# Second attention: exponentials as f16 halves, turned by transposing DMAs, with scores in three pairs of banks

## The reference, cut to what matters

```
x = x + tanh(g_xattn[1]) * L1(layernorm(x), ctx, ctx, wq, wk, wv)
L1: Q, K, V = split(q @ wq.T), split(k @ wk.T), split(v @ wv.T)     # 16 heads of 32
    scores = einsum('bhqd,bhkd->bhqk', Q, K) / sqrt(32)             # 154 keys, no mask
    out    = einsum('bhqk,bhkd->bhqd', softmax(scores), V)          # no output matrix
```

## Time and profile before

| | us |
|---|---|
| median of 3 runs | 2781.3 |
| the profiled execution | 2809.87 |
| its span, first to last instruction | 2808.1 |
| first maximum of the second attention (line 842) | starts 1651.68 |
| last maximum | starts 1965.54 |
| first matmul of the stage behind | starts 1982.32 |

### The profile page before, as it was taken

How to read it: one execution, slowest core, us unless ns; L and a number is a source line. 1 busy time by engine, 2 the same in 40 slices (tenths; PEclk the granted TensorE clock), 3 DMA queues, 4 the chain that set the end, 5 groups by cost and what they waited for, 6 DMA issues and landing times. The chain is left out here.

```text
span 2808.1 us, 44981 instructions
## 1 busy us (share of the span) xinstructions
PE 2644.7 (94%) x16990; PEld 1473.8 (52%) x16990; DVE 1594.4 (57%) x2629; ACT 1425.9 (51%) x3586; POOL 1042.0 (37%) x823
## 2 busy tenths in 40 slices
PE   5999988999999989999999979999999999999999
PEld 3554544444444457777777645565444444444444
DVE  6888885655555346655656568988543422333222
ACT  3888885323222146666666548999443222322221
POOL 1455451465555636666766500111102201221111
PEclk8999999999999999999999989999999999999999
DMA  6221214222222269999999842321420110011000
GB/s 186 52 85 57 74 31 169 61 61 61 75 70 54 76 215 289 285 296 282 288 288 289 207 101 76 91 44 42 157 64 16 46 42 34 16 46 46 19 12 30
DMA packets 287479, 311.17 MB, mean 111 GB/s; under 512 B 155169, under 2 KB 164129, under 8 KB 287265
## 3 DMA queue, kind: packets, MB, share of 16 engines
q1 hardware_dynamic: 250400, 240.96, 27.0%
q0 software_dynamic: 36864, 67.34, 11.7%
HBM read 198.86 MB, written 75.89 MB: 98 GB/s over the span
## 5 line engine op out<-in xcount | busy, mean ns | idle before, releaser
L1376 POOL DMA_INDIRECT ids<-sh_tk,sh_su x256 | 269.8, 1054 | 243.9 <-PE sh_gu L55 70.5
L55 PE MATMUL ex_gu<-ex_xT,ex_h 128*128 128x256 f16 x3072 | 347.5, 273 | 4.6 <-issue 3.8
L55 PEld LDWEIGHTS ex_gu<-ex_xT,ex_h 128*128 128x128 f16 x3072 | 301.2, 98 | 53.9 <-issue 4.4
L1775 POOL DMA_INDIRECT xp<-ex_oo,ex_to x128 | 242.3, 1893 | 178.6 <-ACT ex_oo L1683 123.2
L2323 POOL TENSOR_TENSOR fe_prodT<-fe_pp,fe_prodT 128x512 f16<-128x512 f32 x64 | 77.5, 1210 | 591.2 <-ACT fe_prodT L2108 591.2
L521 PE MATMUL at_g<-id,at_p 128*128 128x128 f32 x1280 | 205.1, 288 | 38.7 <-POOL at_p L901 30.7
L1510 DVE SCALAR_TENSOR_TENSOR ex_h<-ring,ex_h 128x1024 f16<-128x1024 f32 x128 | 151.1, 1222 | 153.0 <-ACT ex_h L1500 153.0
L521 PEld LDWEIGHTS at_g<-id,at_p 128*128 128x128 f32 x1280 | 164.9, 169 | 106.9 <-issue 41.7
L680 ACT ACTIVATE at_s<-at_s,at_mx 128x154 f32<-128x154 f32 x512 | 210.4, 417 | 0.0
L900 POOL TENSOR_TENSOR at_p<-at_s,at_rs 128x1024 f32<-128x1024 f32 x64 | 121.5, 1898 | 223.3 <-DVE at_rs L800 223.3
L55 PE MATMUL at_g<-hm_zT,hm_w 128*128 128x512 f16 x768 | 182.1, 389 | 19.8 <-issue 12.5
(11 more groups left out here) (331 smaller groups left out, 5407.8 us busy)
## 6 DMA issues: line engine op xcount, KB each, us to landing
ring<-L_ffn_expert_gate_up_w SPq DMA_DIRECT2D x64, 1024.0 KB
ring<-L_ffn_expert_down_w SPq DMA_DIRECT2D x64, 512.0 KB
ring<-x SPq DMA_DIRECT2D x24, 1024.0 KB, 5.8
x<-ring SPq DMA_DIRECT2D x16, 1024.0 KB, 4.7
zrows<-hm_zs SPq DMA_DIRECT2D x32, 256.0 KB
xp<-ring SPq DMA_DIRECT2D x8, 1024.0 KB
out<-ring SPq DMA_DIRECT2D x8, 1024.0 KB, 4.3
ring<-xp SPq DMA_DIRECT2D x7, 1024.0 KB, 5.7
```

Of the source, the lines that this page charges most:

```text
L55: mm = nc.tensor.matmul(out, lhs(a, k), rhs(b, k), start=start and i == 0 and j == 0, stop=stop and i == n - 1 and j == 2)
L1376: e.indirect_dma_start(ids, bass.IndirectOffsetOnAxis(slotu[b % 2][:, t, j:j + 1], 0), pair[b % 2][:, t, j, :], None, bounds_check=SLOTS - ...
L1775: e.indirect_dma_start(dst, bass.IndirectOffsetOnAxis(to[:, n:n + 1], 0), o32[y % 2][:, t, :], None, bounds_check=T + SLOTS - 1, oob_is_er ...
```

## The change

Only the second attention is changed (and the semaphores of the two attentions are two sets now).

- The exponentials go to `sc`, f32, all eight heads straight from PSUM. The copy (844) is gone; both maxima are read from PSUM. Scores go round three pairs of banks; `gen` shrinks from four banks to two.
- VectorE makes the high half, `high(i)`: two copies to f16, 128 x 1024 and 128 x 208. It stands after the maxima of unit i+1 and before that step's pieces.
- GpSimd makes the low half: two subtractions, of 128 x 1024 and 128 x 208, with two SBUF inputs.
- SyncE issues two transposing DMAs for each unit, 128 x 1280 f16 each, straight into `pT`. The ten TensorE transposes of a unit and the three copies from PSUM (690, 860) are gone.
- The values are three f16 terms (high by high, high by low, low by high) instead of one f32 product; V and VR are kept in f16 halves, and all four groups of a block stand in phases 7 and 3, two each.

```diff
-        gen = [ps(f"g{i}", [P, 512]) for i in range(4)]
+        gen = [ps(f"g{i}", [P, 512]) for i in range(4 if L0 else 2)]
+        S = ps("S", [P, HH, 256])
+        pairs = [S[:, HG * i:HG * i + HG, :] for i in range(2)]
+        if not L0:
+            pairs.insert(0, maps_ahead.gen[:, :, :].rearrange("p b (k n) -> p (b k) n", n=256))
+        def scores(i, part):
+            return pairs[(2 * i + part) % len(pairs)]
...
-        VALS, FIN = ((7, 8, 11, 12), (13, 13, 14, 14)) if L0 else ((6, 7, 10, 11), (12, 12, 13, 13))
+        VALS, FIN = ((7, 8, 11, 12), (13, 13, 14, 14)) if L0 else ((7, 7, 11, 11), (12, 12, 13, 13))
...
+                        for i in range(unit - NP, unit):
+                            e.wait_ge(*keys_landed(i))
+                    if not L0:
+                        for hv, hp in TERMS:
+                            for j in range(HG):
+                                o = grp * P + j * HD
+                                e.matmul(out[j * HD:(j + 1) * HD, :], V[g][:, hv, o:o + HD],
+                                         ptb[:, hp, place(gi * HG + j), :], start=(hv, hp) == TERMS[0], stop=False)
+                        for hv, hp in TERMS:
+                            mm = e.matmul(out[:, :], VR[g][:, hv, grp, :], ptb[:, hp, HH + gi, :], start=False,
+                                          stop=(hv, hp) == TERMS[-1])
...
-                        e.wait_ge(s["clip"], i)
-                        if not L0:
-                            e.wait_ge(s["expd"], 2 * i - 1)
+                        e.wait_ge(*((s["clip"], i) if L0 else (s["expd"], 2 * i - 1)))
...
-                e.wait_ge(s["expd"], 2 * UNITS - 1)
+                e.wait_ge(s["expd"], 2 * UNITS)
...
+            def high(i):
+                e.wait_ge(s["expd"], 2 * i + 2)
+                if i >= NP:
+                    e.wait_ge(*keys_landed(i - NP))
+                e.tensor_copy(first_keys(prob[i % NP][:, 0, :]), sc[i % NS][:, :, 0:P])
+                e.tensor_copy(last_keys(prob[i % NP][:, 0, :]), rest_of(i)).then_inc(s["p_hi"], 1)
...
+                if not L0 and 0 <= n - behind < UNITS:
+                    e.wait_ge(s["p_hi"], i + 1)
+                    e.tensor_tensor(first_keys(rows[:, 1, :]), sc[i % NS][:, :, 0:P], first_keys(rows[:, 0, :]), ALU.subtract)
+                    e.tensor_tensor(last_keys(rows[:, 1, :]), rest_of(i), last_keys(rows[:, 0, :]), ALU.subtract
+                                    ).then_inc(s["p_lo"], 1)
...
+            def turn_keys(i):
+                if i % TPB == 0 and i // TPB >= 2:
+                    e.wait_ge(s["o_mm"], 2 * (i // TPB) - 2)
+                t = i % TPB
+                for h, made in enumerate(("p_hi", "p_lo")):
+                    e.wait_ge(s[made], i + 1)
+                    e.dma_start_transpose(pT[i // TPB % 2][:, h, :, t * P:(t + 1) * P], prob[i % NP][:, h, :]
+                                          ).then_inc(s[f"keys{i % NP}"], 16)
```

More of the change, by code:

```diff
@@ L262, in __init__ @@
             self.KTn = [sb(f"KT{g}", [P, KT, CTX]) for g in range(BATCH)]
-            self.V, self.VR = [sb(f"V{g}", [P, D]) for g in range(BATCH)], [sb(f"VR{g}", [P, KT, P]) for g in range(BATCH)]
+            half = lambda n, s_: ctx.enter_context(nc.sbuf_tensor(f"at{layer}_{n}", s_, F16))
+            self.V = [half(f"V{g}", [P, 2, D]) for g in range(BATCH)]
+            self.VR = [half(f"VR{g}", [P, 2, KT, P]) for g in range(BATCH)]
     def tensor_keys(self, g, m, out):
@@ L298, in vector_values @@
             heads = lambda rows: rows.rearrange("p g (h n) -> p g h n", h=HG)
-            out = v.tensor_tensor(heads(self.VR[g][:, :, :]), heads(bank.rearrange("p (g m) -> p g m", g=KT)),
-                                  self.mine[:, None, :, None].broadcast_to([P, KT, HG, HD]), ALU.mult)
-        else:
-            out = v.tensor_copy(self.V[g][:, :], bank)
-        out.then_inc(s["v_out"], 1)
+            rows, mine = (heads(bank.rearrange("p (g m) -> p g m", g=KT)),
+                          self.mine[:, None, :, None].broadcast_to([P, KT, HG, HD]))
+            high, low = (heads(self.VR[g][:, h, :, :]) for h in range(2))
+            v.tensor_tensor(high, rows, mine, ALU.mult).then_inc(s["v_hi"], 1)
+            v.wait_ge(s["v_hi"], 3 * g + 2)
+            v.tensor_tensor(low, rows, high, ALU.subtract).then_inc(s["v_hi"], 1)
+            v.wait_ge(s["v_hi"], 3 * g + 3)
+            v.tensor_tensor(low, low, mine, ALU.mult).then_inc(s["v_out"], 1)
+        else:
+            v.tensor_copy(self.V[g][:, 0, :], bank).then_inc(s["v_hi"], 1)
+            v.wait_ge(s["v_hi"], 3 * g + 1)
+            v.tensor_tensor(self.V[g][:, 1, :], bank, self.V[g][:, 0, :], ALU.subtract).then_inc(s["v_out"], 1)
     def scalar_query(self):
@@ L374, in attention @@
     NX = 5
-    NS = 3 if L0 else 2
+    NS = 3
     NP = 2 if L0 else 3
@@ L490, in keys_of, with first_keys, last_keys, rest_of @@
         def keys_of(pb, j):
-            if L0:
-                return pb[:, j * P:(j + 1) * P]
-            if j < HH:
-                return pb[:, :].rearrange("p (n k) -> p k n", k=HH)[:, j, 0:P]
-            return pb[:, :].rearrange("p (n j) -> p j n", j=HH // HG)[:, j - HH, HG * P:]
+            return pb[:, j * P:(j + 1) * P]
+        def first_keys(rows):
+            return rows[:, 0:HH * P].rearrange("p (h n) -> p h n", h=HH)
+        def last_keys(rows):
+            return rows[:, HH * P:].rearrange("p (j r n) -> p r j n", r=HG, n=HD)[:, :, :, 0:REM]
+        def rest_of(i):
+            return sc[i % NS][:, :, P:CTX].rearrange("p (r j) n -> p r j n", r=HG)
+        def keys_landed(i):
+            return s[f"keys{i % NP}"], 32 * (i // NP + 1)
         def part_out(i, part):
@@ L610, in tensor @@
                     piece(*what)
-                if 0 <= i < UNITS:
-                    if not L0:
-                        e.wait_ge(s["expd"], 2 * i + 2)
+                if L0 and 0 <= i < UNITS:
                     keys_turned(i, 4, 1)
@@ L697, in scalar @@
                         exps(n - lag, part)
-                    if part < by_scalar:
+                    if L0 and part < by_scalar:
                         part_copy(n - behind, part)
@@ L840, in vector @@
                         e.wait_ge(s["clip"], i + 1)
-                    else:
-                        e.tensor_reduce(mx[i % 3][:, halves[0]], Sh[0][:, :, 0:CTX], AX.X, ALU.max,
-                                        negate=True).then_inc(s["neg"], 1)
-                        e.tensor_copy(sc[i % NS][:, :, :], Sh[1][:, :, 0:CTX]).then_inc(s["clip"], 1)
+                    for part, half in enumerate(halves):
+                        e.tensor_reduce(mx[i % 3][:, half], sc[i % NS][:, half, :] if L0 else scores(i, part)[:, :, 0:CTX],
+                                        AX.X, ALU.max, negate=True).then_inc(s["neg"], 1)
+                    if not L0:
                         summed(n - lag - 1)
-                        e.wait_ge(s["clip"], i + 1)
-                    for half in halves if L0 else halves[1:]:
-                        e.tensor_reduce(mx[i % 3][:, half], sc[i % NS][:, half if L0 else slice(0, HG), :], AX.X, ALU.max,
-                                        negate=True).then_inc(s["neg"], 1)
                 else:
@@ L852, in vector @@
                 i = n - behind
+                if not L0:
+                    high(i)
+                    for what in plan[n]:
+                        piece(*what)
+                    continue
                 for part in range(by_scalar, 3):
@@ L963, in sync @@
             for n in range(STEPS):
+                if not L0 and 0 <= n - behind < UNITS:
+                    turn_keys(n - behind)
                 for what in sorted(plan[n], key=lambda what: what[0] != "turn"):
@@ L2392, in program @@
         with ExitStack() as own:
-            A = Attention(nc, own, K, I, 0, ring, at_s, I["x"], homes)
+            A = Attention(nc, own, K, I, 0, ring, at0_s, I["x"], homes)
             def sync_first():
```

76 lines of the change are left out of this document (42 added, 34 removed).

## The result

| | before | after |
|---|---|---|
| median of the runs of one comparison | 2785.6 (4 runs) | 2883.6 (2881.3 to 2886.1, 4 runs) |
| ratio of the medians, 95% interval | | 1.035 [1.032, 1.038] |
| in the profiled execution: first maximum of the second attention | 1651.68 | 1634.65 |
| last maximum | 1965.54 | 2025.08 |
| first matmul of the stage behind | 1982.32 | 2058.30 |

The stage is 93.0 us longer, nearly all of the 98 between the medians. (The spans differ less, 2884.1 against 2808.1: in the profiled execution of before everything ahead of this stage took 17.0 us longer; behind it both take 825.8.) The forecast was +46. Of all executions behind this text one slow one, of e9, is left out: 3406 us at a granted clock of 0.742, where the others of e9 had 0.97.

A forecast was written before the change was run, and what follows sets the result against it. No one engine bounds the kernel; TensorE, ScalarE and VectorE are within 10% of the block. Terms 26 - 2 - 4 + 2 + 1 + 12 + 11 = +46 us on 2781.3 gave 2827; range 2764 to 2872.

The forecast's parts named there:

- VectorE's balance and the short phases: VectorE gains 0.75 us a unit without waits; phases 0 and 1 take 3.6 each, 2 5.45, 6 3.7, 7 4.2.
- The port: Phases 2 to 4: VectorE's pieces take turns with GpSimd's subtraction at a shared port, 7.1 us a block.
- the lock doesn't bite: Rival: GpSimd's start slips behind VectorE's pieces or yields; blocks of 37.65, -11 us in all, 2770; 18%.
- half: Rival: the port lock bites half, no clock loss; about +10 us with the end, 2792; 17%.
- Two banks: Phases 4 and 5: the projection waits for the bank of `finish` 0; they become 10.2 and 6.8 us.
- The clock: Phase 4: TensorE's projection runs at the low clock after waits, 2.4 us more; +12 over five blocks.
- low through most of the stage: Rival: TensorE's clock stays low, projections 5.5, phases 0 and 1 7.1; +15 a block, about 2880; 8%.
- SyncE's queue, "under 44.75, so free": A block needs 35.6 us of SyncE's queue, under its 44.75, so the transposing DMAs cost nothing there.
- the transposing DMAs are the bound: Rival: each transposing DMA takes 2.75 us, a block 54 us, +14 seven times; 2890 with the end; 9%.
- Block 6, and the last block: Block 6 keeps the bank wait but not the lock, 35.8 us, -2; the last, 3.35 a unit, 24.2, -4.
- The end: The last transposing DMAs stand behind the next stage's maps, 24 us from block 6's store; +11 (+3 to +16).

The follow-up runs named there:

- e9: Kernel after with finish in phases 4, 5, 6, 6 behind projections, norm's transposes first, maps last, norm's pieces ahead of `high`: 2795.1 us, ratio 1.002.
- e15: Kernel after without GpSimd's large subtraction of the low half (1024 of 1232 elements): 2848.4 us, ratio 1.022.
- e2: Kernel after with the output's transposes (finish) of blocks 0 to 5 in phases 6, 6, 7, 7: 2820.2 us, ratio 1.014.
- e14: Kernel after with 24 extra matmuls keeping TensorE busy in phase 4 of blocks 1 to 6: 2875.0 us, ratio 1.031.
- e1: Kernel after with the norm rows' four transposing DMAs all in phase 5, ahead of the probabilities' DMAs: 2851.5 us, ratio 1.024.
- e6: e5 plus the norm rows' four transposing DMAs in phase 5 ahead of the probabilities': 2810.5 us, ratio 1.009.
- e5: Kernel after with finish in phases 4, 5, 6, 6, in 4 and 5 behind the projection: 2830.6 us, ratio 1.017.
- e11: Kernel after without the low half's transposing DMAs (64 of 128), values using the high half for both: 2862.6 us, ratio 1.027.
- e13: e9 without the low half's transposing DMAs, values taking the high half twice: 2766.2 us, ratio 0.991.
- e4: Kernel after with the next stage's maps and first rows fetched behind the last transposing DMA: 2867.8 us, ratio 1.032.

## Why the prediction was half right

- *VectorE's balance and the short phases*: right. Phases 1, 2 and 6 are within 0.6 of the forecast, phase 7 within 0.9; the large copy takes 0.64 (0.6 taken).
- *The port*: right, 7.1 a block forecast, 5.0 to 6.0 by e15. The rivals "the lock doesn't bite" and "half" fall.
- *Two banks*: right; phase 5 6.63 for 6.8; phase 4 12.36 for 10.2 + 2.4 (which counts the projection as 2.85, having just called it 2.75); e2 removes both waits.
- *The clock*: right in phase 4, 2.4 forecast, 2.5 to 2.7 in e14. It was left out of phase 0 (2.5 a block), and of phases 3 and 5. The rival "low through most of the stage" had part of it: a mean of 0.79 between the levels 0.50 and 1.00 is the low one for 0.42 of blocks 1 to 5. But the 7.1 us that it gave phase 1 didn't come, 3.44 was measured.
- *SyncE's queue, "under 44.75, so free"*: this is the step that failed. It added up the queue's work for a block and compared the sum with the block. The queue is in order and its entries have due times: the norm's third and fourth tile stand behind the DMAs of the unit of phase 5, those behind GpSimd, a store and the late projection. Phase 0 cost 9.7 to 12.2 instead of 3.6, 39 us in five blocks and 6 in block 6. These 45 us are the distance from the forecast's 46 to the 93 of the stage but for 2; that the other misses, between -6 and +6 us each, nearly cancel is luck. e1 and e6 take the wait of phase 0 away by the order alone; e5, with hardly a wait for a `finish` bank, leaves 9.4 of 11.4. The sum itself was nearly right: a transposing DMA holds the queue for 1.34 to 1.55 us where 1.6 was taken, and the repaired kernels, with DMA full, have blocks of 37 to 41 us for its 35.6. The DMA time was taken too low, 1.45 for 1.9 of packet time. The Trainium skill, "Advanced Engine Details and Errata", section "X-Bar Transpose (TRN2)", expects 350 to 400 GB/s; the stretch of e9 with nothing but these DMAs moves 210 GB/s at a DMA share of 1.14, so the trace disagrees.
- *Rival "the transposing DMAs are the bound"*: its 54 us a block and 2890 are the nearest to the 54.7 and 2883.6 measured, but by coincidence. It had every DMA at 2.75 us, and the queue stands waiting for other engines for 117 of 270 us; with half of these DMAs gone 21 of the 93 us go (e11). It is what the repaired kernel runs into (e9 against e13).
- *Block 6, and the last block*: forecast -2 and -4, found +6.3 and +2.1. Block 6 has the same late norm tiles (phase 0 9.9 for 3.6), and its phases 4 and 5 are 1.4 longer each than the 6.8 taken. In the last block most units take 3.8 to 4.04 for the 3.35 taken: TensorE has little to do there, its clock is 0.74 on the mean (before it was 1.00), and the eight scores of a unit last up to 1.41 us instead of 0.81. The window and one unit's scores, after:

```profile
1994.40:2025.10 30.70, 14.26 (x166) 8.55 (x170) 22.93 (x40) 23.80 (x122) 22.54 (x18) 0.74 0.91 155
```
```profile
2004.83 1.41 PE L644 MATMUL at_S<-at_KT,at_qT 32*128 32x154 f32 x16 [2.63 <-ACT at_s L718]
```
- *The end*: the mechanism is right (e4), 16.4 for the 11. The DMAs were taken well: the last values start 25.4 us after the store, forecast 24. What else was missed: before, the last maximum came 2.4 us after the store, now it comes with it; and the cheaper values gave back 1.6 us, not 3.

## What to carry to other kernels

When work moves to an in-order queue, write out the queue's entries in order with the time at which each may start and by which its reader needs it; a sum under the period says nothing of that. Give each shared output bank a reader that is quick at that moment, and let two kinds of work take two banks in turn. When one wait is removed and the time moves by less than the wait, look in the next phase: here what the port had cost in blocks 2 to 6 came back as a wait for DMA, since DMA was full.
